# Ten rounds of graph propagation: two scaled fp16 parts of the value instead of three bf16 parts

## The reference, cut to what matters

```python
def _L3_gnn_ref(feat, src, dst):          # ALPHA = 0.1, K = 10
    deg = segment_sum(ones_like(dst), dst, N)
    norm = where(deg > 0, deg ** (-0.5), 0.0)[:, None]
    feat_0 = feat
    def step(h, _):
        h = h * norm
        h = segment_sum(h[src], dst, N)
        h = h * norm
        return (1.0 - ALPHA) * h + ALPHA * feat_0
    return scan(step, feat, K)
x = layernorm(x + _L3_gnn_ref(x, src, dst))
```

## Time and profile before

| | |
|---|---|
| median of 3 runs | 19704.19 us |
| lowest, highest | 19696.85, 19710.19 us |
| span of the profiled execution | 19689.8 us |
| median of the runs less the span | 14.4 us |
| PE, DVE, POOL, ACT busy over the span | 70%, 57%, 60%, 16% |
| first matmul of the propagation | at 15475.80 us |
| last copy out of `pacc` | at 19648.93 us |
| granted TensorE clock, whole span | 0.778 |

### The profile page before, as it was taken

The page is one execution under the profiler, slowest core; times in us unless marked ns, Lnnn a source line. Parts: engine busy times, 40 slices in busy tenths (PEclk is TensorE's granted clock), DMA queues, the critical chain, the costliest instruction groups (busy, mean ns, idle before and its releaser), DMA issues. The chain is left out here.

```text
span 19689.8 us, 340226 instructions
## 1 busy us (share of the span) xinstructions
PE 13853.8 (70%) x116971; PEld 7768.6 (39%) x116971; DVE 11259.1 (57%) x19905; ACT 3073.8 (16%) x5120; POOL 11826.9 (60%) x10055
## 2 busy tenths in 40 slices
PE   0465555555555588888888466666666699999999
PEld 0344433333333355555555222222222345555554
DVE  2565544444444599999999733333333545555554
ACT  0222222222222111111111011111111000000000
POOL 4788888888888677777777677777777200000000
PEclk6565555555555799999999777777767899999999
DMA  8344444444444432323222255555555345555555
GB/s 308 33 40 37 38 38 38 37 37 38 38 37 37 56 65 64 65 64 65 63 64 64 29 95 89 89 89 89 90 89 80 105 165 200 189 203 199 196 200 176
DMA packets 3778667, 1820.26 MB, mean 92 GB/s; under 512 B 2956641, under 2 KB 3551914, under 8 KB 3758858
## 3 DMA queue, kind: packets, MB, share of 16 engines
q1 hardware_dynamic: 1777244, 1336.91, 25.4%
q0 software_dynamic: 669312, 166.80, 11.7%
q10 hardware_dynamic: 1330864, 300.38, 8.9%
HBM read 1474.43 MB, written 392.90 MB: 95 GB/s over the span
## 5 line engine op out<-in xcount | busy, mean ns | idle before, releaser
L2921 PE MATMUL pacc<-nodes,HB 128*32 128x512 fp8e4 x70560 | 3932.1, 380 | 59.0 <-PEq L2965 59.0
L1991 POOL DMA_INDIRECT xg<-d_tab,s_i x3136 | 3275.0, 1044 | 1077.7 <-issue 940.7
L2526 POOL DMA_INDIRECT xg<-d_tab,s_i x3136 | 2990.4, 954 | 958.1 <-issue 903.1
L2246 PE MATMUL pR<-w,H 128*128 128x384 f32 x6272 | 2388.5, 505 | 669.0 <-PEq L2240 668.6
L1393 POOL DMA_INDIRECT d_acc<-AG,ix x1568 | 2467.6, 1574 | 527.1 <-issue 459.1
L1393 POOL DMA_INDIRECT d_acc<-T,ix x1568 | 2466.6, 1573 | 523.9 <-issue 442.7
L2921 PEld LDWEIGHTS pacc<-nodes,HB 128*32 128x32 bf16 x70560 | 1893.0, 97 | 1971.3 <-issue 74.9
L1746 PE MATMUL pm<-ms,eq 128*128 128x32 f32 x6272 | 1366.0, 399 | 931.1 <-PEq L1744 931.1
L2890 DVE TENSOR_SCALAR nodes<-packed 128x1792 int32<-128x1792 int32 x900 | 944.2, 1049 | 1803.3 <-DVEq L2888 1803.3
L2563 DVE TENSOR_TENSOR_SCAN U<-mU,U,up 128x512 f32<-128x512 f32 x392 | 501.6, 1280 | 2384.0 <-DVEq L2562 2379.3
L1746 PEld LDWEIGHTS pm<-ms,eq 128*128 128x128 f32 x6272 | 1343.8, 330 | 975.2 <-issue 974.8
(11 more groups left out here) (339 smaller groups left out, 18316.4 us busy)
## 6 DMA issues: line engine op xcount, KB each, us to landing
packed<-d_A SPq DMA_DIRECT2D x420, 1792.0 KB
row<-d_m SPq DMA_DIRECT2D x1568, 64.0 KB
xg<-d_tab,s_i POOLq DMA_INDIRECT x6272
wrow<-d_w SPq DMA_DIRECT2D x196, 512.0 KB, 5.4
d_scan<-so ACTq DMA_DIRECT2D x392, 256.0 KB
d_A<-stage ACTq DMA_DIRECT2D x97, 784.0 KB, 10.9
d_ea<-in_ea_t ACTq DMA_DIRECT2D x1, 50176.0 KB, 230.4
d_exp<-T ACTq DMA_DIRECT2D x1, 50176.0 KB, 251.5
```

Of the source, the lines that this page charges most:

```text
L1991: e.indirect_dma_start(out=xg[k][:, t, :], out_offset=None, in_=d_tab, in_offset=bass.IndirectOffsetOnAxis(ap=s_i[n][:, t:t + 1], axis=0)) ...
L2246: last = e.matmul(pR[u % 2][:, j, 0:384], H[k][:, (2 * u + j) * P:(2 * u + j + 1) * P], w2[:, :], start=True, stop=True)
L2526: e.indirect_dma_start(out=xg[n][:, j * ST + c, :], out_offset=None, in_=d_tab, in_offset=bass.IndirectOffsetOnAxis(ap=s_i[d][:, col:col + ...
L2921: end = e.matmul(pacc[k][32 * g:32 * (g + 1), :], HB[i][:, b0 + bb, 32 * h:32 * (h + 1)], of, start=(begins and h == 0), stop=(ends and h ...
```

## The change

The value is given as two fp16 parts of 8192 times the value (`UP`): the rounded product, and what is left of it. The third part is gone, with three of the five VectorE operations in `split` and the tile `hr`. The matmuls for a block go from 12 to 8, for a unit from 84 to 56, and in pass 6 from 294 to 196. The factor that `back4` and `four` carry is divided by `UP`. The degree sums, the loads, the unpacking, the waits between engines and the order of the units are as they were. Lines from L2848 on stand some ten lines higher in the changed file.

```diff
+UP = 8192.0
-            HB = [sb(st, f"HB{i}", [P, NB, 96], BF16) for i in range(2)]
+            HB = [sb(st, f"HB{i}", [P, NB, 64], F16) for i in range(2)]
-            hr = sb(st, "hr", [P, PB, F])
             def split(e, to, blocks, g):
-                n = g.shape[1]
-                e.tensor_copy(to[:, blocks, 0:32], g).then_inc(S("vc"), 1)
+                e.tensor_scalar(to[:, blocks, 0:32], g, UP, None, ALU.mult).then_inc(S("vc"), 1)
                 e.wait_ge(S("vc"), 1)
                 e.sem_inc(S("vc"), -1)
-                e.tensor_tensor(hr[:, 0:n, :], g, to[:, blocks, 0:32], ALU.subtract).then_inc(S("vc"), 1)
...
-                e.tensor_copy(to[:, blocks, 32:64], hr[:, 0:n, :]).then_inc(S("vc"), 1)
...
-                e.tensor_tensor(hr[:, 0:n, :], hr[:, 0:n, :], to[:, blocks, 32:64], ALU.subtract).then_inc(S("vc"), 1)
...
-                return e.tensor_copy(to[:, blocks, 64:96], hr[:, 0:n, :])
+                return e.scalar_tensor_tensor(to[:, blocks, 32:64], g, UP, to[:, blocks, 0:32], ALU.mult, ALU.subtract)
@@ wide_unit
-                    for h in range(3):
+                    for h in range(2):
...
-                                           start=(begins and h == 0), stop=(ends and h == 2))
+                                           start=(begins and h == 0), stop=(ends and h == 1))
@@ last_unit
-                    for h in range(3):
-                        x = (b0 + bb) * 3 + h
+                    for h in range(2):
+                        x = (b0 + bb) * 2 + h
...
-                                       start=(x < 4), stop=(x >= 3 * NB - 4))
+                                       start=(x < 4), stop=(x >= 2 * NB - 4))
@@ four and back4
-                                            BYTE, None, ALU.mult).then_inc(S("vc"), 1)
+                                            BYTE / UP, None, ALU.mult).then_inc(S("vc"), 1)
```

More of the change, by code:

```diff
@@ L2845, in split @@
             def split(e, to, blocks, g):
-                n = g.shape[1]
-                e.tensor_copy(to[:, blocks, 0:32], g).then_inc(S("vc"), 1)
+                e.tensor_scalar(to[:, blocks, 0:32], g, UP, None, ALU.mult).then_inc(S("vc"), 1)
                 e.wait_ge(S("vc"), 1)
                 e.sem_inc(S("vc"), -1)
-                e.tensor_tensor(hr[:, 0:n, :], g, to[:, blocks, 0:32], ALU.subtract).then_inc(S("vc"), 1)
-                e.wait_ge(S("vc"), 1)
-                e.sem_inc(S("vc"), -1)
-                e.tensor_copy(to[:, blocks, 32:64], hr[:, 0:n, :]).then_inc(S("vc"), 1)
-                e.wait_ge(S("vc"), 1)
-                e.sem_inc(S("vc"), -1)
-                e.tensor_tensor(hr[:, 0:n, :], hr[:, 0:n, :], to[:, blocks, 32:64], ALU.subtract).then_inc(S("vc"), 1)
-                e.wait_ge(S("vc"), 1)
-                e.sem_inc(S("vc"), -1)
-                return e.tensor_copy(to[:, blocks, 64:96], hr[:, 0:n, :])
+                return e.scalar_tensor_tensor(to[:, blocks, 32:64], g, UP, to[:, blocks, 0:32], ALU.mult, ALU.subtract)
             def step_sp(e):
@@ L3096, in _ @@
                         e.memset(ones32[:, :], 1.0).then_inc(S("vc"), 1)
-                        e.tensor_scalar(back4[:, :], ident[:, :], BYTE, None, ALU.mult).then_inc(S("vc"), 1)
+                        e.tensor_scalar(back4[:, :], ident[:, :], BYTE / UP, None, ALU.mult).then_inc(S("vc"), 1)
                         e.tensor_scalar(pick4[:, :], ident[:, :].rearrange("p (g x) -> p g x", x=32)[:, :, 0], BYTE, None,
```

## The result

| | before | changed |
|---|---|---|
| median | 19703.81 us (4 runs) | 18463.39 us (4 runs) |
| lowest to highest | 19696.85 to 19710.19 us | 18460.77 to 18471.93 us |
| span of the profiled execution | 19689.8 us | 18458.9 us |
| first matmul of the propagation to last copy out of `pacc` | 4173.1 us | 2942.5 us |

The ratio is 0.9373, 95% interval 0.9362 to 0.9384: 6.3% faster, 1240 us. The forecast of 18461 us was 2 us off, by luck in part. Its span (18447 us) was 12 us short of the measured 18458.9 us. The 14.4 us that it added for what lies around the span were too much by as many: the profiled run of the changed kernel took 18460.9 us, only 2.0 us more than its span, and the rest was scatter of the runs before.

What follows compares the result with a forecast made beforehand. The prediction took TensorE's propagation matmuls as the bound. It summed -1268 + 33 - 6 - 5.6 + 7 - 3 = -1243 us, a span of 18447 us, and forecast 18461 us, range 18415 to 18640 us.

Steps and rivals of the forecast that it cites:

- Term 1: In 60 wide passes TensorE loses 23,520 matmuls of 53.9 ns, if fp16 weights cost what bf16 weights do: -1268 us.
- Term 2: TensorE waits for unit 5 behind `finish` in passes 1 to 5 of nine steps: 45 x 0.73 = +33 us.
- Term 3: Pass 6 loses 2.8 us: nothing gained at five boundaries, -6 us at three loop edges, -5.6 us in steps 1 and 10.
- all queues arrive there earlier: At the loop's three edges all queues reach the jump earlier, so 2 us of each 2.8 were counted: -6 us.
- The 2.8 us in steps 1 and 10: Pass 6's shortening counts in full in these two steps, as nothing follows in the same loop: -5.6 us.
- Term 4: At five step boundaries longer idle time may lower TensorE's clock, 1.45 us each: +7 us (0 to 15).
- The small change: First split ahead of the first matmul shorter, -2 us; short split between step 1 and the loop, -1 us.
- The DMA engines: Rival: unshrunk loads plus instruction packets bind the wide passes, about 18565 us, perhaps 18640 us; chance 0.14.
- The rival of dearer weights: In wide passes fp16 weights cost two passes through the array, 108 ns a matmul, some 20970 us; chance 0.03.
- the path was turned off: The flag after step 1 turns the path off, ten rounds of row gathers follow, far above 30000 us; chance 0.005.
- the matmuls cost less than their number: Another part of the propagation stage binds, for example weight loads, leaving half the gain (19080 us); chance 0.02.

Runs made afterwards that it cites:

- experiment 3: The changed kernel with its two parts in bf16 instead of fp16; propagation 2938.9 us against 2942.5 us.
- Experiment 4: The changed kernel with the second part multiplied and added twice, 84 matmuls a unit again; propagation 4170.2 us, wide pass 64.66 us.
- experiment 1: The changed kernel with `finish` behind unit 5 instead of unit 4 in passes 1 to 5; propagation 2900.5 us against 2942.5 us.
- experiment 2: The changed kernel with three more operations on a scratch tile inside `split`; propagation 3122.2 us against 2942.5 us.
- experiment 11: The kernel before the change with `finish` behind unit 5 in passes 1 to 5; propagation 4169.0 us against 4173.1 us.
- Experiment 5: The changed kernel with `finish` behind unit 5 and five `packed` buffers instead of three; propagation 2878.6 us, against 2900.5 us with three buffers.
- kernel 7: The changed kernel with `finish` behind unit 5, five `packed` buffers and the loop written out; propagation 2841.3 us against 2942.5 us.
- Experiment 8: The changed kernel with only the first of the two parts multiplied; propagation 2414.4 us, wide passes of step 10 34.2 to 36.9 us.
- experiment 6: The changed kernel with `finish` behind unit 5, three `packed` buffers and the loop written out; propagation 2880.6 us, against 2900.5 us with the loop.

## Why the prediction was right

*Term 1, the matmuls that go, -1268 us.* Right. A pass without a wait fell from 64.65 to 43.51 us, 21.14 x 60 = 1268 us. That an fp16 weight costs what a bf16 weight does was the open price in it; experiment 3 shows them equal. What the Trainium skill ("FP8 and Floating Point Precision", TensorE Precision Notes) says of the two types agrees with this. Experiment 4 gives the time back by the number of matmuls alone.

*Term 2, the wait behind `finish`, +33 us.* Right in place and kind (experiments 1, 2, 11), with two wrong factors that nearly cancel. The wait costs 0.90 us a pass and not 0.73: TensorE starts 0.30 us after the unpack's end, where I took 0.14. And only steps 2 to 9 have it in passes 1 to 5, so 40 passes and not 45: step 10's `finish` has no `split`, which the code says and I overlooked. 40 x 0.9 = 36 us.

*Term 3, the boundaries.* Half right. At the five boundaries off the edges nothing was gained in length: pass 6 and the next pass 0 were 76.3 us together on average and are 56.4, a saving of 19.9 us where the matmuls of the wide pass alone make 21.1. Experiment 5 shows the load as cause. At the three edges I took 6 us off, and nothing came of it: 83.6, 84.6 and 83.2 us became 63.9, 62.8 and 64.1, a saving of 20.2 on average. The step that failed is "all queues arrive there earlier": they do, but the wait for instructions grew from 6.5 to 11.9 us. The 2.8 us in steps 1 and 10 came as said (12.8 to 10.1, 9.3 to 6.6).

*Term 4, the clock, +7 us.* Right: it fell at all five boundaries off the edges, where it had stayed at 1.00 before, and these five are 6 us longer together. All eight boundaries, pass 6 and pass 0 less a wide pass, took 115.6 us before and 124.6 after: +9 us, where terms 3 and 4 had +1. The 8 us between the two are the edges: -6 us forecast, +3 measured.

*The small change, -3 us.* The first matmul comes 11.51 us after VectorE's first instruction of the stage (15464.02 to 15475.53), 13.38 before (15462.42 to 15475.80). These 2 us came as said; the third, for the short split between step 1 and the loop, is within the scatter and not shown.

The sum with these sizes is -1268 + 36 + 9 - 5.5 - 3 = -1231.5 us. The spans differ by 1230.9 us. The agreement is closer than the few us by which the propagation scatters.

*The rivals.* The DMA engines did not become the bound at two parts. They stand at 0.83, and in kernel 7, with TensorE never waiting, at 0.86. Experiment 8 shows how near they are: about 35 us to a pass of 43.5. The rival of dearer weights is refuted by experiment 3. That the path was turned off, or that the matmuls cost less than their number, is refuted by the 43.51 us of a pass in step 10 and by experiment 4.

*What stays open.* Why TensorE's wait after the loop's jump grew from 6.5 to 11.9 us. The jump is the cause of the wait, by experiment 6, and neither loads nor VectorE are, by experiment 5. The trace tells more than the experiments. The queue named q8 carries instruction packets of 16 KB; they went from 608 to 420 in the propagation, as TensorE's instructions did, so I take it to be TensorE's. Its packets within the wait at the first edge, before (16830.75 to 16837.27 us) and with the change (16450.29 to 16462.22 us), as packets, MB and share of 16 engines:

```profile
q8 instruction: 1, 0.02, 1.1%
```

```profile
q8 instruction: 3, 0.05, 1.7%
```

Before, the one packet starts 3.5 us after TensorE has run out of work, and TensorE starts 1.9 us after it has landed. With the change two packets come first, at 0.5 and 3.1 us, and the one behind which TensorE starts 1.8 us later comes only at 9.1 us. All three edges of each kernel look like this, within 0.8 us. Each packet takes 1.0 to 1.4 us in both, so they are not slower beside the busy DMA engines. Experiment 4, with 84 matmuls a unit again, has one packet and a wait of 6.4 to 6.6 us. So the longer wait goes with two more packets and with the length of the loop's body in instructions. Why these two are fetched first was not tried.

## What to carry to other kernels

When the work of the bounding engine shrinks by a third, look at each block of work on its neighbours that has a fixed number of units as its cover: the cover shrinks with the units, though the neighbour's average load is far from full. Moving such a block one unit on in the queue can cost nothing and give it all back. A longer wait at TensorE can cost more than its length: behind 39 of 40 waits of 2.97 us the matmuls ran at the lower clock for a while, and behind waits of 0.7 and 1.3 us they did not. Two waits at one place hide each other, so remove both before judging either.

## What the runs showed of the hardware

- TensorE's granted clock stayed at 1.00 after idle times of 0.7 us in each pass and 1.3 us at a boundary. It stood at 0.50 to 0.54 after 2.97 us (39 times out of 40), 4.20 and 6.52 us.
- fp16 and bf16 weights of 128x32 against fp8 data of 512 columns: 381 ns mean length both.
- A scalar_tensor_tensor with f32 and f16 operands of 128x512 took 0.69 us, no less than a tensor_tensor on f32; a tensor_scalar from f32 to f16 took 0.43 us, as the cast to bf16 did.
- After the loop's backward jump TensorE waited 6.4 to 6.6 us in the kernels with 84 matmuls a unit and 11.6 to 12.1 us in those with 56. Written out, the same places have 4.0 to 4.9 us (with three buffers) and 0.7 us (with five). The stretch around the first edge of the changed kernel, with transfers at 337 GB/s beside it:

```profile
16449.00:16462.00 13.00, 1.29 (x48) 0.98 (x40) 6.19 (x6) 0.39 (x1) 0.00 (x0) 0.66 0.93 337
```
